# Second layer of a four-layer sequence kernel: the slot numbers that order the work of four engines are replaced by another set

## The reference, cut to what matters

```python
xa = _ln(x, ln1_w, ln1_b)
sx = jnp.concatenate([state[:, 1:2] - xa[:, :1], xa[:, :-1] - xa[:, 1:]], axis=1)
xxx = jnp.tanh((xa + sx * maa_x) @ maa_w1).reshape(b, l, 5, DM)
xxx = jnp.einsum('blfd,fde->blfe', xxx, maa_w2)
xm = xa[:, :, None] + sx[:, :, None] * (maa_stack + xxx)
...
def step(s, rkvw):
    r_t, k_t, v_t, w_t = rkvw
    a = k_t[..., :, None] * v_t[..., None, :]
    out = jnp.einsum('bhi,bhij->bhj', r_t, u * a + s)
    s = a + w_t[..., :, None] * s
    return (s, out)
...
x1 = x + og * g @ Wo.T
...
rr = jax.nn.sigmoid(xr2 @ Wfr.T)
kk = jnp.square(jax.nn.relu(xk2 @ Wfk.T))
return x1 + rr * (kk @ Wfv.T)
```

## Time and profile before

| | us |
|---|---|
| median of 3 runs | 4489.82 |
| lowest and highest of the 3 | 4485.55, 4512.29 |
| the profiled execution's own time | 4488.23 |
| its span | 4486.2 |

### The profile page before, as it was taken

The page is one execution under the profiler, slowest core; times in us unless marked ns, Lnnn a source line. Parts: engine busy times, 40 slices in busy tenths (PEclk is TensorE's granted clock), DMA queues, the critical chain, the costliest instruction groups (busy, mean ns, idle before and its releaser), DMA issues. The chain is left out here.

```text
span 4486.2 us, 70632 instructions
## 1 busy us (share of the span) xinstructions
PE 4194.8 (94%) x22096; PEld 3153.8 (70%) x22096; DVE 2937.5 (65%) x6494; ACT 1967.5 (44%) x3814; POOL 1576.6 (35%) x1082
## 2 busy tenths in 40 slices
PE   7999999678999997699999999999999999999998
PEld 3444444356777774488887797887887977988866
DVE  5666665268888886376774775766776756757642
ACT  3555555222333321355553455552555543555522
POOL 1222233145555653133233333233332334332230
PEclk7999999789999998899999999999999999999999
DMA  1000000200000000222222322222222222221123
GB/s 39 25 21 28 20 20 15 118 5 10 15 15 15 15 10 19 68 72 67 68 62 74 97 62 80 63 71 69 92 62 73 66 69 88 62 76 58 56 80 131
DMA packets 127596, 241.95 MB, mean 54 GB/s; under 512 B 17012, under 2 KB 38260, under 8 KB 126080
## 3 DMA queue, kind: packets, MB, share of 16 engines
q1 hardware_dynamic: 125152, 234.82, 16.5%
q0 software_dynamic: 1008, 3.67, 0.2%
q10 hardware_dynamic: 1200, 0.52, 0.0%
HBM read 221.91 MB, written 16.78 MB: 53 GB/s over the span
## 5 line engine op out<-in xcount | busy, mean ns | idle before, releaser
L1918 POOL TENSOR_TENSOR c_wl<-c_wr,c_wh 128x512 fp32r<-128x512 f32 (+1 forms) x576 | 820.3, 1436 | 1697.2 <-ACT c_wh L2251 1394.4
L2352 ACT ACTIVATE c_pr<-c_ps,c_nms 128x257 f32<-128x257 f32 x512 | 244.5, 478 | 483.7 <-DVE c_nms L2573 481.7
L581 ACT ACTIVATE a_ex<-a_ps 128x1024 f32<-128x1024 f32 x256 | 261.4, 1024 | 259.5 <-PE a_ps L416 259.5
L692 DVE TENSOR_REDUCE a_nm<-a_ps 128x2 f32<-128x1024 f32 x256 | 311.3, 1220 | 80.9 <-PE a_ps L393 80.8
L1521 DVE TENSOR_TENSOR_SCAN b_sb<-b_wt,b_s,b_ps 128x256 f32<-128x256 f32 x512 | 360.0, 730 | 3.5 <-issue 1.7
L1473 POOL TENSOR_TENSOR b_sb<-b_sb,b_rt 128x1024 f32<-128x1024 f32 x128 | 278.4, 2181 | 185.6 <-DVE b_sb L1521 185.6
L2251 ACT ACTIVATE c_wh<-c_wr 128x512 fp32r<-128x512 f32 (+1 forms) x464 | 315.4, 687 | 48.4 <-PE c_ps L1980 43.5
L1978 PE MATMUL c_ps<-c_hh,c_wh 128*128 128x512 f32 x768 | 310.6, 404 | 12.6 <-DVE c_hl L2457 12.4
L1978 PE MATMUL c_ps<-c_gh,c_wh 128*128 128x512 f32 x768 | 306.7, 399 | 7.2 <-DVE c_gl L2635 4.2
L1980 PE MATMUL c_ps<-c_hh,c_wl 128*128 128x512 f32 x768 | 304.6, 397 | 0.0
L1979 PE MATMUL c_ps<-c_hl,c_wh 128*128 128x512 f32 x768 | 304.1, 396 | 0.0
(11 more groups left out here) (328 smaller groups left out, 10609.1 us busy)
## 6 DMA issues: line engine op xcount, KB each, us to landing
c_wr<-in_downs SPq DMA_DIRECT2D x192, 256.0 KB, 2.6
...
c_wr<-in_wk SPq DMA_DIRECT2D x128, 256.0 KB, 2.9
c_wr<-in_wq SPq DMA_DIRECT2D x128, 256.0 KB, 2.6
...
```

Source lines behind the costliest of these rows:

```text
L581: act.activation(EX[:, n % 4, :, :], ps[:, BT + 2 * (n % 2):BT + 2 * (n % 2) + 2, :], ACT.Exp).then_inc(ex_ready, 1)
L692: dve.tensor_reduce(NM[:, s, :].rearrange("p (h c) -> p h c", h=HG)[:, 2 * p:2 * p + 2, c:c + 1], ps[:, bank:bank + 2, :], AX.X, ALU.max, ...
L1918: pool.tensor_tensor(piece(WL, slot), piece(WR, slot), piece(WH, slot), ALU.subtract).then_inc(piece_cut[slot], 1)
L2352: act.activation(PR[:, i, 0:L + 1], ps[:, BS + 1 - i % 2, 0:L + 1], ACT.Exp, bias=NMS[:, i:i + 1], scale=float(K2) ** -0.5, accum_out=RS[: ...
```

## The change

Every slot number of the four tables may differ; the operations, their operands, the semaphores and the buffers are the same. The slots at which the loops begin and end (`FIRST`, `LAST`) are moved with them. The first lines of the table for TensorE:

```diff
-        PE_AT = dict(spread=-29, gather=3, mean=-178, var=-142, hidden=-122, mix=(-119, -116, -114, -103, -98, -86, -80, -73, -67, -56),
+        PE_AT = dict(spread=-27, gather=8, mean=-139, var=-134, hidden=-118, mix=(-111, -109, -104, -97, -88, -80, -73, -58, -50, -40), k=(-99, -91),
...
-        FIRST, LAST = -186, B * SLOTS + 284
+        FIRST, LAST = -176, B * SLOTS + 292
```

20 lines of the change are left out of this document (10 added, 10 removed).

## The result

The changed kernel takes 4496.31 us in the median of 20 runs, the kernel before 4487.68 in 20 runs beside it: a ratio of 1.0018, with a 95% interval of 1.0011 to 1.0024. So it is 8.6 us slower by the medians. That is inside the predicted range (4464 to 4506) and within 1%, but the forecast was 4484, faster than before, and the whole interval lies on the slower side. The profiled execution took 4498.84 us, 10.6 more than that of before, so its stretches explain the whole of the difference and some 2 us more.

A forecast was written before the change was run, and what follows sets the result against it. TensorE was taken to bound the steady part, VectorE following closely. Terms -1.4 - 4 + 0 - 0.2 = -5.6 us gave 4482.6 from the profiled 4488.23, stated as 4484 because the median lay 1.6 higher; range 4464 to 4506.

The forecast's parts named there:

- The start: First sequence of the second layer: two gains, -1.4 us around g0 and -4 us around the next sequence's v1.
- first term: First sequence: without mean(1) between v1 and g0, the subtraction of mean(1) comes 1 to 1.5 us forward; -1.4 us.
- second term: At v1(1): most of its 3.33 us wait and slow matmuls go, g0 waits about 3; net -4, between 0 and -8.
- (a): fv1, gm0, gm1, gv: waits for VectorE's reading of bank PB stay at 0.6, 0.6 and 0.3 us; change 0.
- (b): hidden, behind VectorE's chain from var: wait 0.0 to 0.3 us where it was 0.4; gain 0.1 us.
- (c): hidden to k0: 11.85 us against 12.4, with a new k0 wait of 0.6 to 0.8; gain 0.7 us.
- (d): k0 to fv1: new waits at two spreads, fk0 and fk1, VectorE standing 4 us at mean2; loss 0.6 to 0.8.
- The sum per period: Steady period: gains and losses cancel to about 0, good to 2 us; six periods 0, from -13 to +13 us.
- The last sequence and the tail: VectorE sets the pace; fk0 starts later, but fk1, fr0, fr1 run with fewer gaps; -0.2 us, between -3 and +4.
- Rival 1: All TensorE waits go in the steady part, plus gains at the start: 4461 us, half of it 4472; chance 18%.
- Rival 2: VectorE falls behind from its stand at mean2, spreads wait, 12 to 25 us slower: 4500 to 4513; chance 17%.
- Rival 3: The new numbers do nothing: waits move one for one to the next place, also at the start; 4490 us, 15%.

The follow-up runs named there:

- a_mean: Changed kernel with the next sequence's mean back between v1 and g0 on TensorE, as before the change; 4500.86 us, ratio 1.0024 to the kernel before.
- a_noshift: Changed kernel with GpSimd's token shift cut to 8 of 256 columns for sequences 1 to 7; 4487.37 us, ratio 0.9998 to the kernel before.
- b_noshift: Kernel before with GpSimd's token shift cut to 8 of 256 columns for sequences 1 to 7; 4484.94 us, ratio 0.9995 to the kernel before.
- a_fk: Changed kernel with VectorE's fkin five slots earlier and TensorE's fk0 four slots earlier; 4489.45 us, ratio 1.0000 to the kernel before.
- a_fk0: Changed kernel with only TensorE's fk0 four slots earlier, VectorE's fkin left in place; 4497.71 us, ratio 1.0031 to the kernel before.

## Why the prediction was wrong

**Where the sum went wrong.** Forecast -5.6 us, measured +10.2 at the layer's end in the profiled executions. Of the difference 7.4 us lie in the start, 2.8 in the periods and 5.9 in the last sequence and the tail; hidden(0) came 0.3 us sooner. The forecast also stood on a median of before of 4489.82 from 3 runs; in 20 runs it is 4487.68.

**The start: -1.4 and -4 predicted, +3.0 and -0.9 measured** (hidden(0) to hidden(1), and hidden(1) to hidden(2)), together 2.0 more in place of 5.4 less. This is the step that failed most. The prediction was right in what goes: the wait of 3.33 ahead of v1(1) is 0.82, and v1(1) takes 3.69. What failed in the first term is "Removing mean(1) from between v1 and g0 [...] brings it only 1 to 1.5 us forward": the mean had covered the wait for v1's bank. Without it g0(0) has 3.56 of pause and 6.53 of product, the first scan comes at 924.56 and not near 921, and the subtraction of mean(1) 2.6 us later than before. In the second term it is "-4, between 0 (if the slow clock only moves to g0)" and the choice within it: the slow clock did move, to g0(1) (5.13). a_mean shows both: with the mean back, hidden(0) to hidden(1) is 3.1 us shorter and hidden(1) to hidden(2) 1.0. The rule of the Trainium skill that the prediction cites, TensorE: Matmul & The Clock Gate, section on HAM oscillation, gave the better second term here, near 0.

**(a)** waits ahead of gm0, gm1, gv: predicted as before (0.6, 0.6, 0.3), measured 0.8, 0.6, 0.4. Right, but for 0.3 in sum.

**(b)** "0.0 to 0.3 wait, it was 0.4. Gain 0.1": measured 1.24. The step that failed is "against 11.9 of work": the prediction took VectorE's durations as fixed, with 1.2 us for the output sum, and did not ask what GpSimd does beside it. From gm0 to hidden it is 0.86 us longer than before, not 0.1 shorter. a_noshift and b_noshift show that the long shift costs 1.48 us a period in the new order, most of it as this collision, and nothing in the old.

**(c)** hidden to k0, 11.85 predicted against 12.4: measured 11.58, of the changed kernel's timeline (the view ends inside the product):

```profile
1276.37 1.99 PE L1078 MATMUL b_ps<-b_xf,b_w 128*128 128x256 f32 x8
```

less 1264.79. Right in size, but k0 hardly waited, where 0.6 to 0.8 were forecast. GpSimd had the input at 1276.31, 4.1 us after the second mix had started, as forecast; the error is in the sum of the work in between. It took 4.2 us and not 3.6, for spreads between short steps cost more than the 0.24 us that were read between two long products: the one behind the second mix 0.51, the two ahead of k0 1.1 together, 0.16 of it waiting for a scan. It is so in a_noshift too, where nothing is late. The waits for L1584 and L1560 went.

**(d)** "Loss 0.6 to 0.8": the waits for scans are 2.6 in sum for five sequences, 0.5 each, and VectorE's stand at mean2 is 4.5 us (I had 4). The other part I had at fk0 and fk1, 0.3 each; the trace has 0.36 ahead of fk1. From k0 to the next gm0 the changed kernel takes 0.55 us longer than before. Right in size.

**The sum per period**, "about 0": without the collision it would have been -0.85, with it +0.62. Both lie in "good to 2 us either way": such a margin, 13 us for six periods, would have covered almost any outcome. (c) and (d) cancelled as forecast, (c) with a wrong term in it. That the total lies inside the range says as little, for the range is 42 us wide.

**The last sequence and the tail: -0.2 predicted, +3.5 and +2.2 measured.** "fk1, fr0 and fr1 run with fewer gaps" is the step that failed, and it had no term for the clock in this stretch. In the changed kernel wo(6) and gv(7) run at the slow clock, 6.38 and 3.62 us instead of 3.72 and 1.91. Part of such a loss comes without any change of order, as b_noshift shows (above), and part is the order's, as the tail and a_fk's median show. The cause of the order's part stays open. What decides whether the clock falls stays open too: wo(6) took 3.72 us in a_fk and 5.41 in a_fk0 behind the same pause of 2.15 and with the gather ahead at full speed in both. In the changed kernel TensorE was at the slow clock already when the pause came: the gather just ahead took 1.94 us, and the granted clock is at its lower level (1.2 GHz) from 1700.8 to 1714.5.

**The rivals.** Rival 1 did not come: the waits ahead of bb0 and the second mix went, and others came. Rival 2, VectorE late, was right in sign and engine but not in place: its stand at mean2 was recovered, and what it could not recover was a stand of 1.5 us in the row without pauses. By the number the lower end of rival 2 (4500) is nearest. Rival 3, waits that only move, describes the start best, where the pause went from v1(1) to g0(1) and 0.9 us were won.
